# Expert rows added in the second preparation, six PSUM banks there, 2 KB store rows, and straight programs in the second attention

## The reference, cut to what matters

```
x = x + delta_rule_attention(layernorm(x))               # layer 0, attention
z = layernorm(x)                                          # layer 0, ffn: a transformer block by itself
z = z + softmax_attention(layernorm(z), 16 heads of 8)
x = x + z + moe(layernorm(z))                             # moe: 8 experts, each token goes to one
# layer 1, attention: 32 heads of 32
h = layernorm(x)
q, k, v = split(h @ w_qkv)                                # w_qkv: 128 x 3072
a = softmax(q k^T / sqrt(32)) v @ w_out + b_out
x = x + layernorm(a) * gamma + beta
x = x + real(ifft(fft(layernorm(x)) @ w_freq)) + bias     # layer 1, ffn
```

## Time and profile before

| | us |
|---|---|
| three runs | 2269.35, 2272.72 (median), 2279.47 |
| the profiled execution | 2269.61 |
| its span, first to last instruction | 2267.9 |
| expert phase ends, second preparation starts | 1012.6, 1013.5 |
| second preparation, last v copy | 1210.6 |
| second attention, first matmul | 1220.4 |

### The profile page before, as it was taken

The page is one execution under the profiler, slowest core; times in us unless marked ns, Lnnn a source line. Parts: engine busy times, 40 slices in busy tenths (PEclk is TensorE's granted clock), DMA queues, the critical chain, the costliest instruction groups (busy, mean ns, idle before and its releaser), DMA issues. The chain is left out here.

```text
span 2267.9 us, 54293 instructions
## 1 busy us (share of the span) xinstructions
PE 1900.0 (84%) x18758; PEld 830.3 (37%) x18758; DVE 1651.5 (73%) x2981; ACT 1222.3 (54%) x2345; POOL 1145.3 (51%) x686
## 2 busy tenths in 40 slices
PE   6467653999999956948997999999999999999975
PEld 3257531222222234633442333333333333333324
DVE  8932565787777655444656888988889888898857
ACT  5321151777777710215662666666666666666655
POOL 8532540000000036331000888888888888888877
PEclk9778776799999966978997999999999999999995
DMA  1210055111111041136886222222222222222201
GB/s 45 48 28 2 0 157 147 35 41 36 34 42 34 19 144 51 52 100 203 284 285 187 61 73 77 76 71 64 74 76 76 72 65 73 76 76 74 64 6 42
DMA packets 239495, 179.62 MB, mean 79 GB/s; under 512 B 59764, under 2 KB 226804, under 8 KB 239108
## 3 DMA queue, kind: packets, MB, share of 16 engines
q1 hardware_dynamic: 230916, 170.02, 26.7%
q0 software_dynamic: 2944, 7.10, 1.1%
q10 hardware_dynamic: 5504, 0.73, 0.2%
HBM read 101.16 MB, written 75.26 MB: 78 GB/s over the span
## 5 line engine op out<-in xcount | busy, mean ns | idle before, releaser
L964 ACT ACTIVATE probs_l<-exp_l 128x512 f32<-128x512 f32 x1024 | 580.2, 600 | 324.0 <-PE exp_l L1013 311.8
L924 DVE TENSOR_REDUCE maxima_l<-max_l 128x1 f32<-128x512 f32 x1024 | 673.8, 685 | 102.1 <-PE max_l L1000 91.3
L901 POOL TENSOR_TENSOR part_sums_l<-probs_l 128x1024 f32<-128x1024 f32 x256 | 622.9, 2433 | 196.9 <-ACT probs_l L964 185.9
L1000 PE MATMUL max_l<-k_stack_l,q_stack_l 96*128 96x512 f16 x1024 | 402.4, 393 | 28.4 <-DVE pv_bank_l L916 10.4
L1013 PE MATMUL exp_l<-q_stack_l,k_stack_l 100*128 100x512 f16 x1024 | 389.5, 382 | 0.1
L1215 DVE TENSOR_REDUCE maxima_l<-max_l 128x2 f32<-128x1024 f32 x256 | 305.6, 1222 | 81.0 <-PE max_l L1298 80.1
L1251 ACT ACTIVATE probs_l<-exp_l 128x512 f32<-128x512 f32 x512 | 282.8, 598 | 118.5 <-PE exp_l L1312 117.3
L1048 PE MATMUL pv_bank_l<-probs_l,v_ring_l 128*32 128x512 f32 x2048 | 273.0, 605 | 0.3 <-issue 0.3
L1000 PEld LDWEIGHTS max_l<-k_stack_l,q_stack_l 96*128 96x128 f16 x1024 | 99.2, 97 | 414.9 <-DVE maxima_l L924 382.6
L1724 POOL IOTA rows_e<- 128x32 int32 x1 | 0.2, 183 | 456.6 <-POOLq L26 456.6
L907 POOL TENSOR_TENSOR part_sums_l<-part_sums_l 128x512 f32<-128x512 f32 x128 | 183.5, 1434 | 10.0
(11 more groups left out here) (277 smaller groups left out, 2573.2 us busy)
## 6 DMA issues: line engine op xcount, KB each, us to landing
scratch_qk_l<-parts_g SPq DMA_DIRECT2D x128, 256.0 KB, 2.2
q_stack_l<-scratch_qk_l SPq DMA_DIRECT2D x192, 128.0 KB, 2.7
k_stack_l<-scratch_qk_l SPq DMA_DIRECT2D x192, 128.0 KB, 2.8
scratch_v_l<-v_g SPq DMA_DIRECT2D x32, 512.0 KB, 3.6
v_ring_l<-scratch_v_l SPq DMA_DIRECT2D x64, 256.0 KB, 2.9
scratch_stack_l<-parts_c SPq DMA_DIRECT2D x96, 128.0 KB, 2.4
q_stack_l<-scratch_stack_l SPq DMA_DIRECT2D x64, 96.0 KB, 2.1
k_stack_l<-scratch_stack_l SPq DMA_DIRECT2D x64, 96.0 KB, 2.1
```

What stands on the lines that cost most here:

```text
L901: pool.tensor_tensor(part_sums[:, i, h, :, :], probs[:, i, h, 0:2, :], probs[:, i, h, 2:4, :], ALU.add).then_inc(pair_sum.sem, 1)
L924: dve.reduce_max(maxima[:, s % 2, at % NT, at // NT:at // NT + 1], max_ps[at % 2][:, :], AX).then_inc(max_taken.sem, 1)
L964: act.activation(probs[:, i, at // NT, at % NT, :], exp_ps[exp_bank(s, at)][:, :], ACT.Exp, scale=a.scale).then_inc(prob_tile.sem, 1)
L1000: pe.matmul(max_ps[at % 2][:, :], qs[0:SHIFT_ROW, s % RING, h, k * P:(k + 1) * P], ks[0:SHIFT_ROW, s % RING, h, :], start=True, stop=True) ...
```

## The change

- The rows of the experts are loaded into `g.y` (the buffer that later takes the attention's output), all eight without a wait, each on its own semaphore `back_in[b]`, which outlives the phase. DVE's additions move into `prep_l1`.
- `prep_l1` is written out. Statistics are taken in five groups of batches (`SUM_GROUPS`); the last three groups, of two batches each, stand in the middle of the q and k tiles of batches 0, 1 and 3. `xn` is made by ACT. The transposes of the next batch stand behind the 13th tile of this one, with two banks for them and both halves of `xnT` used. The ring has six banks. POOL does all powers first, then the memset and the affine_select.
- The scratch of q and k is laid out so that a partition's two parts are 2 KB in one piece; v is stored in two pieces of 1 MB per batch, with 2 KB rows.
- In `attention` DVE, ACT, POOL and SP get straight programs like PE's.

```diff
     for r, parts in enumerate(a.pairs):       # load_group
-                          scratch.qk[side, parts[side], n].rearrange("h d t -> d h t")
+                          scratch.qk[side, n, :, :, parts[side], :].rearrange("h d t -> d h t")
...
 def attention(nc, g, a, scratch, w_out, out, addend):
-        def stream(eng, step):
-            for s in range(U):
-                step(0, s)
-            with eng.Fori(1, B) as turn:
-                for s in range(U):
-                    step(turn, s)
-            for s in range(OUT_LAG):
-                step(B, s)
...
-            stream(dve, step)                 # and pool, act; SP's own loop likewise
+            for n in range(M + OUT_LAG):
+                step(n // U, n % U)
...
 def moe(nc, g, ins, scratch):
             for b in range(B):
-                if b >= 2:
-                    sp.wait_ge(added.sem, added.made(b - 2, 0))
-                sp.dma_start(back[:, b % 2, :, :], scratch.by_token[...]).then_inc(back_in[b % 2], 16)
+                sp.dma_start(g.y[:, b * NT:(b + 1) * NT, :], scratch.by_token[...]).then_inc(g.back_in[b], 16)
...
-            for b in range(B):                # DVE, end of moe
-                dve.wait_ge(summed.sem, summed.made(b, 0))
-                dve.wait_ge(back_in[b % 2], 16 * (b // 2 + 1))
-                dve.tensor_tensor(g.x[:, at, :], g.x[:, at, :], back[:, b % 2, :, :], ALU.add)
...
+SUM_GROUPS = ((0, 1), (1, 2), (2, 4), (4, 6), (6, B))
+MOMENTS_AT = {0: 2, 1: 3, 3: 4}
 def prep_l1(nc, g, ins, scratch):
-        xnT_bank, bank = pb("xnT"), [pb(f"ring{i}") for i in range(4)]
+        xnT_bank, bank = [pb(f"xnT{i}") for i in range(2)], [pb(f"ring{i}") for i in range(6)]
...
         def _(pool):
+            for n in range(len(SUM_GROUPS)):
+                pool.wait_ge(moments.sem, moments.made(n, 0))
+                pool.tensor_tensor(rstd[:, tiles], var_eps[:, tiles], g.minus_half[...], ALU.pow)
             pool.memset(rows, 0.0)
             pool.affine_select(out=rows, in_=rows, ...)
-            with pool.Fori(0, B) as b:
-                pool.wait_ge(moments.sem, moments.made(b, 0))
-                pool.tensor_tensor(rstd[:, :], var_eps[:, :], g.minus_half[:, 0:NT], ALU.pow)
...
         def _(dve):
+            def moments_of_x(n):
+                for b in range(*SUM_GROUPS[n]):
+                    dve.wait_ge(g.back_in[b], 16)
+                    did(dve.tensor_tensor(g.x[:, at, :], g.x[:, at, :], g.y[:, at, :], ALU.add))
+                ...  # bn_stats, bn_aggr, var_eps of the group's tiles
+            def centre(n):
+                dve.wait_ge(rstd_ready.sem, rstd_ready.made(n, 0))
+                dve.scalar_tensor_tensor(out=shift[:, tiles], in0=mv[:, tiles, 0], scalar=-1.0, in1=rstd[:, tiles], ...)
+            moments_of_x(0); centre(0); moments_of_x(1); centre(1)
+            for b in range(B):
                 for i in range(QK_TILES):
+                    if i == QK_TILES // 2 and b in MOMENTS_AT:
+                        moments_of_x(MOMENTS_AT[b])
+                    if i == QK_TILES // 2 + 4 and b in MOMENTS_AT:
+                        centre(MOMENTS_AT[b])
                     dve.wait_ge(part0.sem, part0.made(b, i))
...
         def _(act):
+            normalised(0); transposed(0)      # 4 x activation(Identity) into xn; copy into xnT
+            for b in range(B):
                 for i in range(QK_TILES):
                     act.copy(parts[:, i, 0, :], bank_of(b, i)[:, :])
+                    if i == QK_TILES // 2 and b + 1 < B:
+                        normalised(b + 1)
+                    if i == QK_TILES - 2 and b + 1 < B:
+                        transposed(b + 1)
...
         def _(pe):
+            transposes(0)
+            pe.wait_ge(w_loaded, 16)
+            for b in range(B):
                 for i in range(QK_TILES):
+                    free(b, i - R)            # R = 6 banks: DVE's remainder of tile i-6
                     pe.matmul(bank_of(b, i)[:, :], w[:, i * P:(i + 1) * P], xnT[:, b % 2, :], ...)
+                    if i == QK_TILES - 4 and b + 1 < B:
+                        transposes(b + 1)
...
 def program(nc, ins, out):
+        sem = phase_semaphores(nc, ctx, "_back")      # cleared when the program ends
+        g.back_in = [sem(f"back_in{b}") for b in range(B)]
+        g.y = sb("y", [P, T, D])
```

More of the change, by code:

```diff
@@ L861, in load, with step @@
                 if exists(turn, s, RING):
-                    wait_ge(sp, score_tile.sem, score_tile.made(turn * U + s - RING, TILES - 1), g.passed)
+                    sp.wait_ge(score_tile.sem, score_tile.made(turn * U + s - RING, TILES - 1))
                 load_group(sp, g, a, scratch, turn * U + s, slot)
-            def step(turn, s, more=True):
-                first = isinstance(turn, int) and turn * U + s == 0
-                if more and not first:
+            def step(turn, s):
+                first = turn * U + s == 0
+                if exists(turn, s + 1, 0) and not first:
                     load(turn, s + 1)
@@ L881, in step @@
                                      ).then_inc(shifted[(s - 1) % RING], 16)
-            for s in range(U):
-                step(0, s)
-            with sp.Fori(1, B - 1) as turn:
-                for s in range(U):
-                    step(turn, s)
-            for s in range(U):
-                step(B - 1, s, s + 1 < U)
-            step(B, 0, False)
+            for n in range(M + 1):
+                step(n // U, n % U)
         @block.gpsimd
@@ L946, in step @@
                         dve.wait_ge(y_ps.sem, y_ps.made(n - OUT_LAG, 0))
-                        tiles = bass.ds((turn - 1) * NT, NT)
+                        tiles = slice((turn - 1) * NT, turn * NT)
                         dve.tensor_tensor(out[:, tiles, :], y_bank[:, :].rearrange("p (k d) -> p k d", k=NT), addend(tiles),
                                           ALU.add).then_inc(y_taken.sem, 1)
-            stream(dve, step)
+            for n in range(M + OUT_LAG):
+                step(n // U, n % U)
         @block.scalar
@@ L980, in step @@
                                        scale=-1.0).then_inc(shift_ready.sem, 1)
-            stream(act, step)
+            for n in range(M + OUT_LAG):
+                step(n // U, n % U)
         @block.tensor
@@ L1675, in moe @@
         y_out = [sem(f"y_out{s}") for s in range(DEPTH)]
-        back_in, added = [sem(f"back_in{s}") for s in range(2)], made("added")
         def fill_tails(eng, experts):
@@ L2110, in _, with did, settle @@
-            with dve.Fori(0, B) as b:
-                normalise(b, b)
+            mine = [0]
+            def did(ins_):
+                ins_.then_inc(own, 1)
+                mine[0] += 1
+            def settle():
+                dve.wait_ge(own, mine[0])
+            def moments_of_x(n):
+                tiles = tiles_of(n)
+                for b in range(*SUM_GROUPS[n]):
+                    at = slice(b * NT, (b + 1) * NT)
+                    dve.wait_ge(g.back_in[b], 16)
+                    did(dve.tensor_tensor(g.x[:, at, :], g.x[:, at, :], g.y[:, at, :], ALU.add))
+                settle()
+                for k in range(tiles.start, tiles.stop):
+                    did(dve.bn_stats(stats[:, k, :], g.x[:, k, :]))
+                settle()
+                for k in range(tiles.start, tiles.stop):
+                    did(dve.bn_aggr(mv[:, k, :], stats[:, k, :]))
+                settle()
+                dve.tensor_scalar(var_eps[:, tiles], mv[:, tiles, 1], LN_EPS, None, ALU.add).then_inc(moments.sem, 1)
@@ new lines, in normalised, with transposed @@
+            def normalised(b):
+                act.wait_ge(shift_ready.sem, shift_ready.made(group_of(b), 0))
+                if b >= 2:
+                    act.wait_ge(xnT_ps.sem, xnT_ps.made(b - 2, 0))
+                for k in range(NT):
+                    tile = b * NT + k
+                    act.activation(xn[:, b % 2, k, :], g.x[:, tile, :], ACT.Identity, bias=shift[:, tile:tile + 1],
+                                   scale=rstd[:, tile:tile + 1]).then_inc(xn_ready.sem, 1)
+            def transposed(b):
+                act.wait_ge(xnT_ps.sem, xnT_ps.made(b, 0))
+                if b >= 2:
+                    act.wait_ge(made_ps.sem, made_ps.made(b - 2, QK_TILES + v_cols - 1))
+                act.copy(xnT[:, b % 2, :], xnT_bank[b % 2][:, :]).then_inc(xnT_sb.sem, 1)
@@ L2144, in _, with free @@
+            def free(b, i):
+                if i < 0:
+                    b, i = b - 1, i + QK_TILES + v_cols
+                if b < 0:
+                    return
+                if i < QK_TILES:
+                    pe.wait_ge(part1.sem, part1.made(b, i))
+                else:
+                    pe.wait_ge(v_sb.sem, v_sb.made(b, i - QK_TILES))
+            transposes(0)
+            pe.wait_ge(w_loaded, 16)
+            for b in range(B):
                 pe.wait_ge(xnT_sb.sem, xnT_sb.made(b, 0))
```

150 lines of the change are left out of this document (68 added, 82 removed).

## The result

| | before | after |
|---|---|---|
| median of the runs (range) | 2271.92 (2269.35 to 2279.47), 4 | 2242.41 (2237.46 to 2244.06), 4 |
| profiled execution, span | 2269.61, 2267.9 | 2243.36, 2241.7 |

The ratio is 0.9863, 95% interval 0.9846 to 0.988: 1.4% faster. The forecast was 2249.

The account below looks back on a forecast made before the run. It took latency to bound the second preparation's start, and PE the rest of that preparation and the second attention. Terms: -20.8 - 5.6 + 3.0 - 0.3 + 0.5 = -23.2 us, forecast 2249; 8 in 10: 2241 to 2259.

Parts of the forecast that it names:

- Part 2, the turns: Turns of the second preparation: -5.6 us from PE's waits for the copy, +3.0 from DVE's statistics.
- Part 1, the start: From the experts' end to the first q matmul: 20.8 us earlier, released by the weights' load; ends 23 and 17.
- seven waits of 0.80: PE's 0.80 us wait for ACT's copy of `xnT` in each preparation turn goes seven times: -5.6 us.
- PE waits for DVE in the groups: DVE's three statistics groups take 4.2 us each against slack of 3.2, so PE waits 1.0 us three times: +3.0.
- the wide rows at nothing: The preparation's 2 KB store rows save DMA share but no time, since nobody waits for a store.
- ACT's activations at nothing: Four activations, 1.65 us in all, added to ACT in each preparation batch lie within the slack and cost nothing.
- Part 3, straight programs -0.3: In the second attention, straight programs save only 0.09 us of register work at the addition: -0.3 for all, ends -2.6 and 0.
- Part 4: At the program's end, clearing `back_in` adds one more clearing and meeting of the engines: +0.5 us, ends 0 and 1.0.
- Deeper gain: Rival, chance 0.14: PE never waits for DVE's statistics, attention turns lose their 0.37 us, start at its fast end: 2242 us.
- Late centring: Rival, chance 0.10: POOL's memset holds the last group's `shift` on DVE some 5.5 us, PE 5: 2254 us.
- Slower: Rival, chance 0.03: straight attention programs stall on instruction fetch; at 0.82 us a group on PE, 2295 us.
- less than it says: Rival, chance 0.05: expert rows not ready or powers still late at the preparation's start; half its gain gives 2259 us.

Follow-up runs that it names:

- late transposes: The changed kernel with PE's transposes and ACT's copy of `xnT` back at the end of each batch, behind the v tiles and copies; median 2253.0 us.
- old rows: The changed kernel with store rows of 1 KB for q and k and 512 bytes for v, four v stores a batch; median 2239.8 us.
- before, fills last: The kernel before with only POOL's memset and affine_select moved behind its eight powers; median 2276.2 us, ratio 1.0013 to before.

## Why the prediction was right or wrong

The step that failed is the sum of Part 2, the turns: -5.6 + 3.0 = -2.6 was forecast and -6.4 measured, 3.8 of the 6.6 us by which the medians' gain passed the forecast's. The mechanism of both terms was right and both sizes were off, each so that the gain came out too small. Of the rest, 0.7 is the start's and 0.3 the straight programs'; what is left is scatter.

Part 1, the start: right. 21.5 us against 20.8, released by the weights' load, as drawn; the mean over the nine executions with this start is 14.2 us and the gain 21.4. The two transfers on that path were off against each other: the last rows landed 10.0 us after their first issue and not 8.9, and the weights released PE 4.0 us after that and not 5.8. (The terms of DVE's path add up to 4.0 us and not to "some 4.1", which changes nothing.)

Part 2, "seven waits of 0.80": the mechanism right, the term too small. It is 1.06 a turn, 7.4 and not 5.6. I took only the wait that the row names. The transposes themselves cost 0.60 by their row, which I left where it was; but among other matmuls they delay the next one by 0.43 only. Start to start of the neighbours, 1056.47 - 1055.07 = 1.40 in the earlier trace rows, was the number to take, and 0.97 of it goes; the late transposes show 0.99.

Part 2, "PE waits for DVE in the groups": right in kind and place, too large. 0.43 three times and not 1.0. DVE stands for 3.76 us and not 4.2 (additions back to back 0.64 each, no settling wait seen at 0.15 each). The slack of 3.2 was nearly right: 3.76 - 0.43 = 3.33. The two terms are off by 1.8 and 1.7; mended, they give -7.4 + 1.3 = -6.1. The marks give 6.3; 0.1 of the rest is in the last batch, and the first ran 0.4 us less at clock 0.50.

Part 2, the wide rows at nothing, DMA share below 0.87: right, 0.76, and shown by the old rows. ACT's activations at nothing: right for this kernel. But the move of `xn` to ACT was not free of worth, if my reading of "before, fills last" holds.

Part 3, straight programs -0.3: right within 0.4; 0.6 over seven turns. Part 4: the tail grew by 1.0, which I can't tell from scatter (61.4 to 63.7 over all kernels).

The rivals. "Deeper gain" had 2242, which is the time measured, and that is luck: of its three reasons only the start came near (21.5 of its 22.8); PE does wait for DVE in the groups, and a turn of the attention gives 0.09 and not 0.37. Late centring fell, with 0.15 us beside the memset; the account that its rows gave was the right one. "Slower" fell with turns of 119.24 us in straight programs, and "less than it says" with the start.

What no step had, -3.2 in turn 0 and +3.2 ahead of the change, nearly cancel here and are scatter, the first traced to a meeting and a fall of the clock. The known stages give -21.4 - 6.1 - 0.6 = -28.1, which from a median of 2272 gives 2244; the runs' 2242 to 2243 lie 1 to 2 us from it.

## What to carry to other kernels

Price a wait by the start-to-start time of its neighbours, not by the bracket in its row: what stands in front of the wait changes its own cost when it is moved between other work. Before moving a long fill on POOL, look at what DVE does in the place that it moves to: the same 14 us were free beside remainders from PSUM and cost 15.6 us beside a `tensor_scalar`, 3.0 of them through PE's clock. And look at what SP issues last in a phase: thirteen short issues that nobody waited for by name were the largest gain left, 7.5 us.

## What the hardware showed unexpectedly

One program's turn 0 of the attention takes 168.7 or 171.5 us (168.2 to 171.9 over all). A tenth of a microsecond in the start of one DVE instruction decides whether it takes 0.7 or 2.5 us, and when PE's clock came back to 1.00, ten microseconds earlier, goes with that start in all fourteen executions. And each long POOL instruction holds a `tensor_scalar` on DVE for itself: the one issued 0.15 us behind the memset caught the next, so that four instructions of 1.1 us in all took 14.56.
